# Two score-maximum rounds in one slot, each PSUM bank waited for by itself, and the stages behind them four slots forward

## The reference, cut to what matters

```
# 0: additive attention over the 77 text tokens
rho = (tanh(ctx @ Ws [:,None] + xn @ W [:,:,None] + b) * w).sum(-1) + mask
x += tanh(g0) * FiLM(xn, softmax(rho) @ ctx)          # two tanh of projections
# 1: linear layer with a low-rank part
x += tanh(g1) * (ln(x) @ W.T + bias + ln(x) @ L.T)
# 2: attention with 16 heads of 16 over the same 77 text tokens
scores = q @ k.T / 4                                  # (heads, 1024, 77)
x += tanh(g2) * (softmax(scores) @ v) @ Wo + bo
# 3: 16 experts in 4 groups (best 2 groups, then best 4 experts), and 2 shared ones
x += tanh(g3) * (sum_k tw_k * expert_k(ln(x)) + shared(ln(x)))
```

## Time and profile before

| | |
|---|---|
| median of three executions | 1582.64 us (1576.61 to 1583.19) |
| the profiled execution | 1580.62 us |
| span of its trace, first to last instruction | 1578.9 us |
| mean granted TensorE clock over the span | 0.928 of full speed (2.4 GHz) |
| TensorE matmuls busy | 1296.2 us, 82%, 11876 instructions |
| ScalarE busy | 1080.9 us, 68%, of it 774.3 us tanh of the scan (1232) |
| VectorE busy | 951.1 us, 60% |
| GpSimd busy | 529.8 us, 34% |
| DMA | 207.59 MB, mean 131 GB/s |

### The profile page before, as it was taken

How to read it: one execution, slowest core, us unless ns; L and a number is a source line. 1 busy time by engine, 2 the same in 40 slices (tenths; PEclk the granted TensorE clock), 3 DMA queues, 4 the chain that set the end, 5 groups by cost and what they waited for, 6 DMA issues and landing times.

```text
span 1578.9 us, 34591 instructions
## 1 busy us (share of the span) xinstructions
PE 1296.2 (82%) x11876; PEld 761.8 (48%) x11876; DVE 951.1 (60%) x2301; ACT 1080.9 (68%) x1781; POOL 529.8 (34%) x505
## 2 busy tenths in 40 slices
PE   5777787787688999998999899989997886898860
PEld 2212242333225554655475546554666575577750
DVE  7986647635743775387438854895468865223323
ACT  4998886777887899878987897769872441222220
POOL 1101121121453221425543445256434434404216
PEclk8878997999799999999999999999998997899995
DMA  7654502503122343454444553534346554669954
GB/s 214 224 195 114 125 1 67 139 1 86 68 86 74 96 122 87 102 167 134 142 113 128 147 145 112 141 96 155 100 128 187 155 134 129 174 183 237 258 172 120
DMA packets 234433, 207.59 MB, mean 131 GB/s; under 512 B 121945, under 2 KB 191137, under 8 KB 234273
## 3 DMA queue, kind: packets, MB, share of 16 engines
q1 hardware_dynamic: 210017, 160.29, 37.8%
q0 software_dynamic: 12288, 33.57, 6.5%
q10 hardware_dynamic: 11968, 11.54, 2.3%
HBM read 110.01 MB, written 70.16 MB: 114 GB/s over the span
## 4 chain that ended last, share of the span: by engine, by line
PE 48%; ACT 21%; DVE 18%; issue 7%; POOL 4%; DMA 1%; another core or an unknown queue 1%; SPq 0%; POOLq 0%; DVEq 0%; ACTq 0%
ACT tanh_tiles L1251 17%; PE psF L1020 8%; PE psE L866 6%; PE psE L868 5%; PE psE L867 5%; PE psY L866 3%; PE psY L868 3%; PE psY L867 3%; PE psF L866 2%; PE psF L867 2%; PE psF L868 2%; PE psF L872 2%; POOL work L852 2%; PE psF L1190 1%; DVE xn L1457 1%
## 5 line engine op out<-in xcount | busy, mean ns | idle before, releaser
L1251 ACT ACTIVATE tanh_tiles<-feat,text_bias 128x512 f32<-128x512 f32 x1232 | 774.3, 713 | 77.9 <-DVE feat L1627 58.2
L1020 PE MATMUL psF<-tanh_tiles,wslide 128*32 128x512 f32 x2464 | 367.6, 652 | 60.4 <-ACT tanh_tiles L1251 59.0
L1656 DVE TENSOR_TENSOR tile<-tile,psE 128x512 f32<-128x512 f32 x128 | 87.5, 683 | 165.2 <-ACT tile L1278 87.7
L799 POOL TENSOR_TENSOR hid<-tile,hid 128x512 f16<-128x512 f32 x76 | 88.4, 1164 | 231.8 <-ACT hid L1270 231.0
L823 POOL DMA_INDIRECT xs_rows<-xs,slot_i x128 | 127.5, 996 | 115.2 <-PE psF L1020 43.6
L1270 ACT CAST hid<-tile 128x512 f16<-128x512 f32 x128 | 78.5, 613 | 119.8 <-DVE tile L1656 114.0
L866 PE MATMUL psY<-down,hid 128*128 128x256 f16 x512 | 143.0, 279 | 18.5 <-issue 12.7
L1278 ACT ACTIVATE tile<-psE 128x512 f32<-128x512 f32 x128 | 75.6, 591 | 115.7 <-PE psE L868 65.6
L866 PE MATMUL psE<-xg,gate_hi 128*128 128x128 f16 x768 | 147.1, 224 | 7.7 <-issue 6.7
L866 PE MATMUL psE<-xg,up_hi 128*128 128x128 f16 x768 | 147.4, 221 | 6.4 <-issue 5.2
L867 PE MATMUL psE<-xg,up_hi 128*128 128x128 f16 x768 | 147.3, 221 | 6.3 <-issue 6.1
(11 more groups left out here) (311 smaller groups left out, 2840.9 us busy)
## 6 DMA issues: line engine op xcount, KB each, us to landing
down<-down_split SPq DMA_DIRECT2D x208, 256.0 KB
y_rows<-hid SPq DMA_DIRECT2D x52, 256.0 KB
xs_rows<-peakT SPq DMA_DIRECT2D x24, 512.0 KB, 6.6
y_rows<-tanh_tiles ACTq DMA_DIRECT2D x44, 256.0 KB
down_split<-hid SPq DMA_DIRECT2D x18, 256.0 KB, 3.3
xscan<-in_x SPq DMA_DIRECT2D x8, 512.0 KB, 5.8
x<-in_x SPq DMA_DIRECT2D x8, 512.0 KB, 5.2
w_lin<-w_split SPq DMA_DIRECT2D x15, 256.0 KB
```

The lines of the kernel that those rows point to most:

```text
L799: pool.tensor_tensor(hid_lo[:, n], tile[:, v.n % 2], hid_hi[:, n], ALU.subtract).then_inc(glo_done, 1)
L1020: last = pe.matmul(psF[32 * j:32 * j + 32, RHO, :], wslide[:, c, 31 - g:63 - g], tanh_tiles[:, st.at(SETS, 2 * g + c) % HRING, j], start=g ...
L1251: act.activation(tanh_tiles[:, n % HRING, j], feat[:, c], ACT.Tanh, bias=text_bias[:, c, col:col + 1]).then_inc(h_ready, 1)
L1656: dve.tensor_tensor(tile[:, n], tile[:, n], psE[:, (2 * v.n + 1) % 3], ALU.mult).then_inc(g_done, 1)
```

## The change

Two rounds stand in each of the slots 22 to 25: the even one opens the slot on TensorE and on VectorE, the odd one stands at the end of the slot, where all rounds stood. The product's code moves into `peak_product`, the maximum's into `peak_maximum`. Each of the two matmuls of a round now raises `peak_ps` itself, VectorE reduces each bank with an instruction of its own (four heads, 308 columns), and a bank's next matmul waits for that bank's maximum alone; both semaphores count 16 a tile instead of 8.

`PEAKT` and all later stages of the front come four slots earlier, with them the first four phases of the next scan's prelude (three slots earlier: 45, 46, 48, 49 for 48, 49, 51, 52; the copy of the features stays in 53), and the copy of the normalised rows on GpSimd (43 for 47). The slots without tanh move along: from step 0 on four sets go from slots 27 to 30 to the slots 48 to 51 that later stages had, or stood near; the last set's slot stays 51. Step 1's own list moves likewise. No instruction of any other stage changes.

```diff
--- before.py
+++ after.py
@@ -39,20 +39,20 @@
 
 SLOTS = 3 * EX
 SOFT, FILM, KV, KVN, X1, LN2, LN2T, LIN, LN3, LN3T, QPROJ, PEAK, PEAKT, SCORES, PV, OT, WO, LN4, LN4T, ROUTE = (
-    1, 5, 7, 5, 6, 7, 12, 13, 14, 18, 20, 22, 30, (31, 36), (35, 40), 42, 43, 45, 48, 50)
-PEAK_SLOTS = [PEAK + u for u in range(NT * KC)]
+    1, 5, 7, 5, 6, 7, 12, 13, 14, 18, 20, 22, 26, (27, 32), (31, 36), 38, 39, 41, 44, 46)
+PEAK_SLOTS = [PEAK + u // 2 for u in range(NT * KC)]
 SCORE_SLOTS = [first + k // 2 for first in SCORES for k in range(PCH)]
 ROUTE_SLOTS = [ROUTE, ROUTE + 2, ROUTE + 3]
 CHOOSE = 4
 
 NORM1, NORM1T, FEAT, COPY = 0, 3, 5, 6
-PRELUDE = [48, 49, 51, 52, 53]
+PRELUDE = [45, 46, 48, 49, 53]
 PRELUDE0 = [42, 43, 45, 47, 53]
 PHASES = [NORM1, NORM1 + 1, NORM1T, FEAT, COPY]
 
 
-BUSY = (10, 12, 18, 20, 31, 32, 33, 36, 37, 42, 48)
-BUSY1 = (2, 12, 22, 24, 26, 28, 29, 31, 32, 33, 37)
+BUSY = (10, 12, 18, 20, 27, 28, 29, 32, 33, 38, 44)
+BUSY1 = (2, 12, 22, 23, 24, 25, 27, 28, 29, 32, 33)
 TANH_SLOTS, TANH_SLOTS1 = ([i for i in range(1, SLOTS - 2) if i not in busy][:SETS] for busy in (BUSY, BUSY1))
 KV0 = 20
 KV_AT = {0: 0, 1: 1, 2: 2, 7: 3}
@@ -84,7 +84,7 @@
 ROWS_G = BLOCKS * P
 WORDS = NPAIR
 PLACE = 4
-XS = 47
+XS = 43
 SCATTER = 6
 XGRING = 3
 COMB = 5
@@ -1055,8 +1055,25 @@
                                 pe.wait_ge(rhoT_ready, st.at(1, 0))
                         rho_set(st, s // 2, s % 2)
 
+            def peak_product(u, s, st):
+
+                t, c = u // 2, u % 2
+                if u == 0:
+                    pe.wait_ge(q_lo, st.at(2, 2))
+                    if st.half == 0 and st.batch() in AHEAD:
+                        pe.wait_ge(kv_loaded, 128 * (AHEAD.index(st.batch()) + 1))
+                    if s in KV_AT:
+                        pe.wait_ge(kv_lo, 9 * (KV_AT[s] + 1))
+                for hf in range(2):
+                    if u:
+                        pe.wait_ge(peak_used, st.at(16, 2 * u + hf - 1))
+                    pe.matmul(psF[:, hf, 0:PH], qT_hi[:, c, t * P:(t + 1) * P],
+                              K_hi[:, c, hf * PH:(hf + 1) * PH], start=True, stop=True).then_inc(peak_ps, 1)
+
             def slot(i, s, sc, st):
                 T = s * SLOTS + i
+                if st and i in PEAK_SLOTS:
+                    peak_product(2 * (i - PEAK), s, st)
                 for b in range(2):
                     v = began(T, DOWN + b)
                     if v and v.y_ps:
@@ -1144,23 +1161,10 @@
                     for c in range(KC):
                         product(psF[:, c], [(Wqh[:, k, c * P:(c + 1) * P], Wql[:, k, c * P:(c + 1) * P],
                                              xT_hi[:, k], xT_lo[:, k]) for k in range(KC)]).then_inc(q_ps, 1)
-                for u in range(8):
-                    if i == PEAK_SLOTS[u]:
-                        t, c = u // 2, u % 2
-                        if u == 0:
-                            pe.wait_ge(q_lo, st.at(2, 2))
-                            if st.half == 0 and st.batch() in AHEAD:
-                                pe.wait_ge(kv_loaded, 128 * (AHEAD.index(st.batch()) + 1))
-                            if s in KV_AT:
-                                pe.wait_ge(kv_lo, 9 * (KV_AT[s] + 1))
-                        else:
-                            pe.wait_ge(peak_used, st.at(8, u))
-                        for hf in range(2):
-                            last = pe.matmul(psF[:, hf, 0:PH], qT_hi[:, c, t * P:(t + 1) * P],
-                                             K_hi[:, c, hf * PH:(hf + 1) * PH], start=True, stop=True)
-                        last.then_inc(peak_ps, 1)
+                if i in PEAK_SLOTS:
+                    peak_product(2 * (i - PEAK) + 1, s, st)
                 if i == PEAKT:
-                    pe.wait_ge(peak_used, st.at(8, 8))
+                    pe.wait_ge(peak_used, st.at(16, 16))
                     for t in range(NT):
                         last = pe.transpose(psF[0:32, 0, t * P:(t + 1) * P], peak[:, t, :], ident[:, :])
                     last.then_inc(peakT_ps, 1)
@@ -1633,8 +1637,18 @@
                     for n in range(len(staged) * i // (SLOTS - 3), min(len(staged) * (i + 1) // (SLOTS - 3), len(staged))):
                         split_expert(n)
 
+            def peak_maximum(u, st):
+
+                for hf in range(2):
+                    dve.wait_ge(peak_ps, st.at(16, 2 * u + hf + 1))
+                    heads = HC * (u % 2) + HC // 2 * hf
+                    dve.tensor_reduce(peak[:, u // 2, heads:heads + HC // 2],
+                                      psF[:, hf, 0:PH].rearrange("p (h t) -> p h t", t=TXT), AX, ALU.max).then_inc(peak_used, 1)
+
             def slot(i, s, sc, st):
                 T = s * SLOTS + i
+                if st and i in PEAK_SLOTS:
+                    peak_maximum(2 * (i - PEAK), st)
                 v = began(T, ADD)
                 if v and not v.routed and v.f:
                     add_shared(v, 0)
@@ -1782,12 +1796,8 @@
                             dve.tensor_copy(qT_hi[:, c], xn_t[:, c]).then_inc(q_hi, 1)
                         dve.wait_ge(q_hi, st.at(2, c + 1))
                         dve.tensor_tensor(qT_lo[:, c], xn_t[:, c], qT_hi[:, c], ALU.subtract).then_inc(q_lo, 1)
-                for u in range(8):
-                    if i == PEAK_SLOTS[u] + D_PEAK:
-                        dve.wait_ge(peak_ps, st.at(8, u + 1))
-                        dve.tensor_reduce(peak[:, u // 2, HC * (u % 2):HC * (u % 2 + 1)].rearrange("p (b h) -> p b h", b=2),
-                                          psF[:, 0:2, 0:PH].rearrange("p b (h t) -> p b h t", t=TXT), AX,
-                                          ALU.max).then_inc(peak_used, 1)
+                if i in PEAK_SLOTS:
+                    peak_maximum(2 * (i - PEAK) + 1, st)
                 if i == PEAKT:
                     fr.link(dve.tensor_tensor(xt, xt, bo_row[:, :].unsqueeze(1).to_broadcast([P, NT, D]), ALU.add))
                 for m in range(2 * PCH):
```

## The result

1626.9 us (median, 1625.66 to 1628.22) against 1582.91: a ratio of **1.0288** (95% interval 1.0261 to 1.0315), slower. The forecast was 1585, its range 1564 to 1605. The profiled execution has a span of 1623.8 us, 44.9 more than before.

The account below looks back on a forecast made before the run. It took TensorE to bound steps 4 to 7, while step 1 waits for chains, as steps 2 and 3 still do. Terms -5.55, +13.95 and -5.7 gave +2.7 on 1580.62, 1583; the median's 2.0 made 1585, range 1564 to 1605.

Parts of the forecast that it names:

- Boundaries and round 0: Steps 4 to 7: TensorE stands 0.91 us at each of three pair boundaries (2.7) and 1.1 for the query's low half.
- the rival of the late maxima: VectorE reaches odd maxima late in slots 22 to 25; boundaries grow by 0.7, adding 8 us: 1593; chance 0.15.
- Queues passed: Other work on SP and GpSimd that moved stages pass: nothing, or up to 3 us once on SP; nothing on GpSimd.
- the forecast of -5.7: Step 8's term: earlier comparisons and subtraction -3.0, rounds ending 3.7 earlier, 1.0 given back to unit products among the scores.
- unit products among the scores: Steps 2 and 8: products of the units come to stand among the moved scores, +1.0 us in each.
- The end of a step: Steps 4 to 6: TensorE stands 3.05 us before FEAT instead of 2.4, for the next scan's low halves: +0.65 each.
- Step 7's tanh waits: At step 7's end, with four tanh sets moved there, TensorE waits set by set: +2.0 us.
- The clock: Rival: waits near 2.7 us halve TensorE's clock, two 1.7 us stretches a step in steps 3 to 7: 1602; chance 0.15.
- a sign that it is wrong: The prediction called itself wrong if steps 4 to 7 don't lengthen or the clock leaves 1.00 in them.
- The subtraction: Softmax's subtraction on VectorE no longer meets GpSimd's ranking, 0.49 us instead of a median 1.79: -1.3 a step.
- Steps 1 to 3: Steps with chain waits, shortened by the earlier stages: -1.7, -3.5 and -0.35, together -5.55 us.

Follow-up runs that it names:

- e2: The changed kernel with the gathers of combined rows in steps 6 and 8 one slot later; 1617.33 us, 1.0182 of the kernel before.
- e4: The changed kernel with the stages behind the rounds moved three slots instead of four and the gathers two slots later; 1601.34 us, 1.0084 of the kernel before.
- e3: The changed kernel with the next scan's product FEAT in slot 51 instead of 49; 1.0246 of the kernel before.
- e7: e4 with the even round's product in the middle of TensorE's slot instead of at its head; 1.0019 of the kernel before.
- e12: e7 with the product FEAT in slot 51 instead of 49; 1583.05 us, 0.9974 of the kernel before.
- e8: e4 with the high halves of the next scan's rows copied by VectorE in all steps instead of by ScalarE; 1.0113 of the kernel before.
- e10: The kernel before with the gathers of steps 6 and 8 four slots later, made to meet the scores' last low halves; 1.0127 of the kernel before.

## Why the prediction was wrong

- **Boundaries and round 0** (2.7 + 1.1 a step): right. 0.87 against 0.91 a boundary, 0.472 against 0.48 a half maximum, the low half's wait 1.2 in step 5 (1.1), and the pairing alone cost 1.0%, 16 us, against 15.2 over four steps. Of the twelve boundaries in steps 4 to 7 one, in step 6, waited 1.5 instead of 0.44, with the maximum late: the rival of the late maxima took 1 us, not 8.
- **Queues passed** is the step that failed. It read "On GpSimd ... nothing", and looked at the scatters and low weights, not at the gathers of steps 6 and 8. They put 5.5 and 6.0 us more of PV's wait there, and behind three of these four waits the clock fell: 1.1% (17 us) by e2. In step 8 the forecast of -5.7 turned into +11.0; the early part held (from the SiLU of its first unit to that of the fifth 28.2 instead of 32.4), and the scores lost it: it is 4.7 shorter without the collision (e2), and 7.6 more with three slots instead of four (e4), 1.3 below before.
- **The four-slot move had no term for the units' period** in steps 4 to 7, and 1.0 each in steps 2 and 8 for unit products among the scores. "The stages behind the rounds come four slots earlier" was counted as time, not as a place: units begin every three slots, so each stage met another one of their products. One slot less is worth 1.0% (e2 to e4); which waits make it up stays open, and since three and four slots alone were tried, that it is the period and not the shorter move is argued, not shown.
- **The end of a step** (+0.65): mis-sized. The wait was 3.5, not 3.05, so 1.1 more than the 2.4 before, and the half clock after it (1.7) wasn't in the term. Step 7's tanh waits grew by 2.4 (forecast 2.0). In e3, where FEAT stands later, TensorE waits for tanh instead, so a part of this is ScalarE's; moving FEAT gave no gain clear of noise there, and 0.45% on e7 (e12).
- **The clock** was the slower rival, and half right: it fell behind long waits, not at the boundaries. Steps 4 to 7 had 0.95 to 0.99 instead of 1.00, which the prediction named as a sign that it is wrong. Over the rounds of step 4 it stayed at 1.00 (two of the three boundaries lie in this stretch; it was 1.00 at the first, at 605.0, too):

```profile
606.00:625.00 19.00, 17.96 (x110) 6.09 (x108) 9.04 (x17) 15.38 (x23) 3.80 (x4) 1.00 0.46 101
```

So the rule of the Trainium skill (TensorE: Matmul & The Clock Gate, "A second HAM failure mode: psum-queue depth-cycling") doesn't describe these short waits. Nor did the rival's own condition, a wait of about 2.7, decide: behind one of 3.5 in step 6 of the changed kernel and behind e4's three of 2.7 the clock stayed at 1.00, behind e8's three of 2.4 it fell.
- **The subtraction** (-1.3 a step): its size was right, 0.49 in all steps; how much of it reached the step's time no run isolates in steps 4 to 7.
- **Steps 1 to 3**: -4.2 measured, -5.55 forecast. Step 2 alone differs by 4.7 between the kernel before and e10, which are the same up to step 6, so the agreement may be luck.

The range stopped at 1605 because no rival was about the other work that the moved stages meet.

## What to carry to other kernels

When a stage moves in a hand-written schedule, list for its new slots every instruction on every queue, those of rare steps too: here gathers of four indirect DMAs in two of eleven steps cost about as much as the pairing of the eight rounds that was the point (1.1 and 1.0%). Look also at the period of the work beside the moved stages: three slots, the units' period, were 1.0% better than four. That a shift by a whole period is better in general one pair of runs doesn't show. Two instructions with a round trip between them are worth separating by any work that is there anyway.

## What the runs showed of the hardware

From step 4 up to 1340 us of the changed kernel's trace eight TensorE waits were 3.5 us or longer. Behind seven of them the granted clock was at 0.5 (1.2 GHz) for 2.7 to 5.5 us, behind one of 3.5 it stayed at 1.00; across the runs the length of a wait alone doesn't tell which comes (2.7 without a fall in e4, 2.4 with one in e8). The three waits of 0.44 among the rounds of step 4 left it at 1.00. The four indirect DMAs of a gather took 4.7 us of GpSimd's queue in step 8 (1285.21 to 1289.94), some 1.26 from one start to the next.
